# Residual rows and scattered expert additions go straight to an output declared with spare rows, without a scratch sum

## The chip, the cores and the metric

One core of one Trainium2 chip runs the kernel. The metric is the device time of one execution in microseconds (us), as a median of several runs; lower is better.

## The reference

A decoder layer on x of 2 x 1024 tokens with 256 features: a decayed linear attention, a cross attention over 154 context rows with 16 heads, and a mixture of experts. Only the end of the last part matters for this change:

```python
h   = layernorm(x)                         # x: 2048 rows x 256, after both attentions
g   = softmax(h @ gate_w.T)                # 8 experts; the two largest of g + gate_b are taken
out = x + shared_expert(h)                 # silu((h@sw1+sb1)*(h@sw3+sb3)) @ sw2 + sb2
for each token, for each of its 2 experts e:
    out[token] += g[token, e] * expert_e(h[token])
```

The result has 2048 rows of 256 f32, 2.10 MB.

## The kernel before

The kernel is written by hand: each engine has its own program (`@block.tensor`, `.scalar`, `.vector`, `.gpsimd`, `.sync`), and semaphores order them. The layer runs in stages. Up to about 410 us the attentions and the shared expert run; x stays in SBUF and collects their sums, in four chunks of 512 tokens.

The experts work by sorted rows. GpSimd (POOL) scatters the normalised row of each token twice, once for each of its experts, into the scratch DRAM tensor `xs` (L1502), where each expert has a region of its own. With a row go its token number and its gate weight. Places without a token are filled from a table of pad rows that carry numbers from 2048 upwards, so that what is computed for them lands in spare rows. The tensor `zs` in DRAM has ZROWS = 2048 + 8*128 + 7*128 = 3968 rows of 1 KB: 2048 for the tokens and 1920 spare ones.

`zs` is filled first. SP's queue copies x with the shared expert's part into it, one 512-row chunk a time (`base`, L1665; chunks 0, 1, 2 on semaphore `base_zs`, chunk 3 on `base_zs3`), and gives the spare rows some finite content from the input (L1681).

Then NS = 39 tiles of 128 sorted rows follow each other, `s` = 0 to 38, the first NA = 16 of them made from the first three chunks. For each tile SP reads 128 rows from `xs` (`read`, L1672, up to NR = 8 tiles ahead, held back by the landing of the addition eight tiles earlier, L1671); TensorE (PE) transposes (L689), multiplies with both first weights (L700), transposes the hidden rows (L710) and multiplies with the second weight (L720); VectorE (DVE) adds biases (L1421, L1425, L1436) and multiplies with the gate weight (L1439) into one of four buffers `sY`; POOL adds the 128 rows to `zs` with one indirect DMA that reads, adds and writes (L1583).

Two such additions may meet in a row of `zs` when they belong to two experts. So the addition of tile s waits for the landing of s-2 always, and for that of s-1 where the expert changes between the two (the value `need`; always for s = 1, 2 and 16). The landings count on two semaphores in turn, `to_zs[s % 2]`. DVE waits for the landing of s-4 before it refills `sY`.

When the last two additions have landed, SP (L1729) and ACT (L963) copy half of the 2048 rows each from `zs` to the output `out`, and ACT waits for both copies. That is the end of the kernel.

Of the kernel before, what the change touches and what calls it, by code (L numbers as in the profile page):

```python
# [7 lines left out]
ALU = mybir.AluOpType  # L8
ACT = mybir.ActivationFunctionType
AX = mybir.AxisListType  # L10
F32 = mybir.dt.float32
U8 = mybir.dt.uint8
I32 = mybir.dt.int32
U32 = mybir.dt.uint32

P = 128
B = 2
S = 1024
D = 256
N = B * S  # L20
NT = N // P
NCH = 4
CT = 512
# [9 lines left out]
NS = (2 * N + NE * (P - 1)) // P  # L33
# [3 lines left out]
ZROWS = N + NE * P + 7 * P  # L37
NU = NT // 2
NR = 8
# [118 lines left out]
    return v.rearrange("p (a n) -> p a n", a=1).broadcast_to([P, n, NE])  # L158


def decoder(nc, A, xs, zs, out):
    with ExitStack() as ctx:
        def sb(name, shape, dt=F32):
            return ctx.enter_context(nc.sbuf_tensor(name, shape, dt))

        def sem(name):
            return ctx.enter_context(nc.semaphore(name))
# [9 lines left out]
        x = sb("x", [P, NT, D])  # L177
# [80 lines left out]
        xsl = R2[:, 0:NR * XW].rearrange("p (s n) -> p s n", s=NR)  # L258
# [21 lines left out]
        sY = R1[:, 11264:12288].rearrange("p (s n) -> p s n", s=4)  # L280
# [18 lines left out]
        in_row = [sem(f"in_row{i}") for i in range(NR)]  # L299
        to_xs = sem("to_xs")  # L300
        pad_xs = sem("pad_xs")
        base_zs = sem("base_zs")
        base_zs3 = sem("base_zs3")
        to_zs = [sem(f"to_zs{i}") for i in range(2)]
        to_out = sem("to_out")

        zeroed = signal("zeroed", ["ones", "cnt", "pad0", "pad1"])
        stat = signal("stat", [(kc, i, n) for kc in NORMS for i in range(4) for n in range(2)])
# [33 lines left out]
        def added(s):  # L342

            return 16 * (s // 2 + 1)
# [397 lines left out]
        def _(e):  # L742
            w = Waits(e)
# [212 lines left out]
                if s >= 1:  # L956
                    hidden_turned(s - 1)

            half = N // 2
            outr = out.rearrange("b s d -> (b s) d")  # L960
            for s in (NS - 2, NS - 1):
                e.wait_ge(to_zs[s % 2], added(s))
            e.dma_start(outr[half:N, :], zs[half:N, :]).then_inc(to_out, 16)  # L963
            e.wait_ge(to_out, 32)

        @block.vector
        def _(e):
            w = Waits(e)
# [462 lines left out]
            def results(s):  # L1431
                u = bank["y", s]
                w.wait_ge(full[u.i], u.filled)
                if s >= 4:
                    w.wait_ge(to_zs[s % 2], added(s - 4))
                e.tensor_tensor(sY[:, s % 4, :], pb[:, u.i, 0:D], eb[:, bass.ds(b_reg[s] * 960 + 2 * F, D)], ALU.add  # L1436
                                ).then_inc(free[u.i], 1)
                w.wait_ge(free[u.i], u.drained)
                e.tensor_scalar(sY[:, s % 4, :], sY[:, s % 4, :], xsl[:, s % NR, D + 1:D + 2], None, ALU.mult  # L1439
                                ).then_inc(*yrow.next(s))  # L1440

            for s in range(NS + 2):
                if s < NS:
                    hidden(s)
                if s == 0:
                    shared_out(3, 1)
                if s >= 2:
                    results(s - 2)
                if s == 2:
                    late_ends()  # L1450
                if s == 3:
                    late_jumps()
                if s == 4:
                    late_slots()

        @block.gpsimd
        def _(e):
            w = Waits(e)
# [42 lines left out]
            def scatter_rows(c, k, i):  # L1501
                e.indirect_dma_start(  # L1502
                    out=xs, out_offset=bass.IndirectOffsetOnAxis(ap=pos[:, c, k, i:i + 1].bitcast(U32), axis=0),
                    in_=xn[:, NORMS.index((3, c)) % 2, i, :], in_offset=None).then_inc(to_xs, 16)
# [31 lines left out]
            d = bank["mix", 3, 1]  # L1536
# [30 lines left out]
                scatter_rows(3, 0, i)  # L1567
            second_weights(3)

            w.wait_ge(base_zs, 64)  # L1570
            for s in range(NS):
                w.wait_ge(slots.sem, slots["early" if s < NA else "late"])
                v = e.value_load(need[0:1, s:s + 1], min_val=16, max_val=16 * (NS + 4)) if s not in (0, 1, 2, NA) else None  # L1573
                w.wait_ge(yrow.sem, yrow[s])
                if s >= 2:
                    w.wait_ge(to_zs[s % 2], added(s - 2))
                if s in (1, 2, NA):
                    w.wait_ge(to_zs[(s - 1) % 2], added(s - 1))
                elif s:
                    e.wait_ge(to_zs[(s - 1) % 2], v)  # L1580
                if s == NA:
                    w.wait_ge(base_zs3, 16)
                e.indirect_dma_start(  # L1583
                    out=zs, out_offset=bass.IndirectOffsetOnAxis(ap=xsl[:, s % NR, D:D + 1].bitcast(U32), axis=0),
                    in_=sY[:, s % 4, :], in_offset=None, compute_op=ALU.add).then_inc(to_zs[s % 2], 16)
                if s < 4:
                    scatter_rows(3, 1, s)

        @block.sync
        def _(e):  # L1590
            w = Waits(e)
            xv = A["x"].rearrange("b (t p) d -> p (b t) d", p=P)

            def fetch_side(t):
                s = t % 2
                if t >= 2:
                    d = bank["s", t - 2, 2, 0]
                    w.wait_ge(free[d.i], d.drained)
                e.dma_start(fs[:, s, :, :], A["fside"][t]).then_inc(in_fs[s], 16)

            def fetch_mask(t):
                s = t % 2
                if t >= 2:
                    w.wait_ge(masked.sem, masked[t - 2, heads_of(t - 2)[-1]])
                else:
                    for q in range(4):
                        d = bank["div", 3, q]
                        w.wait_ge(full[d.i], d.filled)
                e.dma_start(mk[:, s, :, :], A["mask"][t]).then_inc(in_mk[s], 16)
# [32 lines left out]
            for key in (("con", B - 1, 2), ("pj", 3, "q", 1)):  # L1642
                d = bank[key]
# [7 lines left out]
            def fetch_w2():  # L1651
                for ex in range(NE):
                    e.dma_start(ew2[:, ex * 768:ex * 768 + 512].rearrange("p (k n) -> p k n", k=2),
                                A["L0_ffn_w2"][ex, 0:256].rearrange("(k p) n -> p k n", p=P)).then_inc(in_ew2, 16)
                    e.dma_start(ew2[0:96, ex * 768 + 512:ex * 768 + 768], A["L0_ffn_w2"][ex, 256:352]
                                ).then_inc(in_ew2, 16)

            def fetch_eb(lo, hi):
                e.dma_start(eb[:, lo * 960:hi * 960], A["ebias"][:, lo * 960:hi * 960].broadcast_to(
                    [P, (hi - lo) * 960])).then_inc(in_ew, 16)  # L1660

            def base(c, to):
                d = bank["so", c, 1, 1]
                w.wait_ge(free[d.i], d.drained)
                e.dma_start(zs[c * CT:c * CT + CT, :].rearrange("(t p) d -> p t d", p=P),  # L1665
                            x[:, 4 * c:4 * c + 4, :]).then_inc(to, 16)

            def read(s):
                if s >= NR:
                    w.wait_ge(to_zs[s % 2], added(s - NR))  # L1670
                v = e.value_load(sei[0:1, 1, s:s + 1], min_val=0, max_val=XROWS - P)  # L1671
                e.dma_start(xsl[:, s % NR, :], xs[bass.ds(v, P), :]).then_inc(in_row[s % NR], 16)  # L1672

# [2 lines left out]
            for t in range(NT):  # L1676
                if t >= 2:
                    fetch_side(t)
                fetch_mask(t)
                if t == 4:  # L1680
                    e.dma_start(zs[N:ZROWS, :], A["x"].rearrange("b s d -> (b s) d")[0:ZROWS - N, :]  # L1681
                                ).then_inc(base_zs, 16)
                if t == 13:
                    base(0, base_zs)

            for r in range(2):
                d = bank["s", NT - 1, 2, r]
# [2 lines left out]
            fetch_w13(0, 3)  # L1690
            w.wait_ge(masked.sem, masked[NT - 1, (0, H)])
            fetch_w2()
            base(1, base_zs)
            fetch_eb(0, 3)
            w.wait_ge(scaled.sem, scaled[NT - 1, 1])
            fetch_w13(3, 6)
            d = bank["pT", 7, 1, 4]
            w.wait_ge(full[d.i], d.filled)
            fetch_w13(6, NE)
            for i in range(2):  # L1700
                for r in range(2):
                    d = bank["av", 7, 1, i, r]
# [5 lines left out]
            w.wait_ge(slots.sem, slots["early"])  # L1708
            for s in range(NR):
                read(s)  # L1710
            base(2, base_zs)
            w.wait_ge(prows.sem, prows[0])
            for ex in range(NE):
                v = e.value_load(prow[0:1, ex:ex + 1], min_val=ex * RG, max_val=ex * RG + N)
                e.dma_start(xs[bass.ds(v, P), :], A["pad"][ex * P:(ex + 1) * P, :]).then_inc(pad_xs, 16)
            base(3, base_zs3)
            for s in range(NR, NA):
                read(s)
            w.wait_ge(slots.sem, slots["late"])
# [2 lines left out]
            for s in range(NA, NS):  # L1722
                read(s)

            half = N // 2
            outr = out.rearrange("b s d -> (b s) d")
            for s in (NS - 2, NS - 1):
                w.wait_ge(to_zs[s % 2], added(s))
            e.dma_start(outr[0:half, :], zs[0:half, :]).then_inc(to_out, 16)  # L1729


def layout(inputs):
# [64 lines left out]
```

## Time and profile before

| | us |
|---|---|
| three runs | 605.31, 605.50, 607.53 |
| median | 605.5 |
| the profiled execution's own time | 605.35 |
| its span in the trace (first to last instruction or landing) | 603.5 |
| granted TensorE clock over the span, share of full | 0.991 |

Busy shares of the span: PE 94%, DVE 73%, ACT 52%, POOL 39%. The page cuts the span into 40 slices of 15.1 us; a digit is the busy share of a slice in tenths. The chain of work that ended last is followed back from the end; "issue" in it is time in which an engine waited for nothing that the profile shows. POOLq, SPq and ACTq are the sequencers of these engines, on which DMAs are issued.

### The profile page before, as it was taken

The page shows a single profiled execution, that of the slowest core. Times are in us where ns is not written, and L with a number is a line of the kernel's source. Part 1 is how long each engine was busy: PE and PEld are TensorE (multiplying, and loading weights), DVE is VectorE, ACT ScalarE, POOL GpSimd, SP SyncE. Part 2 cuts the span into 40 slices and gives each one's busy share as a digit, 9 for nine tenths or more (in the row PEclk, how much of TensorE's full clock was granted, in tenths as well). Part 3 has the DMA queues.
Part 4 walks back from the last instruction along what each step waited for, and adds up shares of the span by engine and source line. Part 5 has one row for each costly group of instructions (what it writes and reads, how often), then busy time and mean ns, then how long its engine had stood idle before and what let it go on. Part 6 is the DMA issues. An engine that isn't in the chain of part 4 may idle for free.

```text
span 603.5 us, 11032 instructions
## 1 busy us (share of the span) xinstructions
PE 569.9 (94%) x3625; PEld 434.0 (72%) x3625; DVE 437.6 (73%) x817; ACT 311.7 (52%) x985; POOL 234.3 (39%) x227
## 2 busy tenths in 40 slices
PE   4999999999999999999999999999999999999990
PEld 2546657787788878688787868777777777777770
DVE  3999999999686979749697498566575555555550
ACT  2642424388869794877959569424233232322320
POOL 2010010227453745367342684262354334333341
PEclk9999999999999999999999999999999999999996
DMA  9910004246250502415133149764544343443425
GB/s 305 364 46 2 1 1 167 87 166 236 106 207 5 194 18 93 153 35 211 36 115 123 45 146 304 240 247 121 136 96 71 57 68 62 62 71 54 63 28 163
DMA packets 36647, 71.00 MB, mean 118 GB/s; under 512 B 5184, under 2 KB 29472, under 8 KB 34080
## 3 DMA queue, kind: packets, MB, share of 16 engines
q1 hardware_dynamic: 28272, 59.18, 29.7%
q0 software_dynamic: 7152, 9.34, 9.3%
q10 hardware_dynamic: 1168, 1.78, 0.9%
q8 instruction: 30, 0.49, 0.3%
q14 instruction: 25, 0.20, 0.1%
HBM read 58.86 MB, written 17.48 MB: 126 GB/s over the span
## 4 chain that ended last, share of the span: by engine, by line
PE 35%; DVE 23%; issue 17%; DMA 14%; POOL 5%; ACT 2%; POOLq 2%; DVEq 0%; SPq 0%
DMA zs_dram<-R 13%; PE pb L571 7%; DVE R L1035 6%; PE pb L471 6%; PE pb L521 4%; PE pb L606 4%; PE pb L488 4%; PE pb L537 4%; DVE R L1058 3%; PE pb L618 2%; DVE R L1013 2%; DVE mx L1121 1%; POOLq L1573 1%; PE pb L541 1%; DMA xs_dram<-xn,pos 1%
## 5 line engine op out<-in xcount | busy, mean ns | idle before, releaser
L819 ACT ACTIVATE R<-R,mx 128x154 f32<-128x154 f32 x256 | 104.3, 414 | 0.0
L700 PE MATMUL pb<-R 128*128 x312 | 98.8, 460 | 0.3 <-ACT R L932 0.3
L1583 POOL DMA_INDIRECT zs_dram<-R x39 | 60.6, 1553 | 96.2 <-DMA zs_dram<-R 51.0
L936 ACT ACTIVATE R<-R 128x352 f32<-128x352 f32 x39 | 19.4, 497 | 116.7 <-DVE R L1429 110.8
L700 PEld LDWEIGHTS pb<-R 128*128 128x128 f32 x312 | 56.2, 190 | 25.4 <-issue 0.6
L471 PE MATMUL pb<-xnT,wq 128*128 128x256 f32 x256 | 58.0, 383 | 0.0
L720 PE MATMUL pb<-R 128*128 (+1 forms) x234 | 57.0, 380 | 0.0
L810 ACT ACTIVATE R<-pb,bq 128x256 f32<-128x256 f32 x64 | 30.0, 473 | 49.7 <-PE pb L471 49.7
L471 PEld LDWEIGHTS pb<-xnT,wq 128*128 128x128 f32 x256 | 47.8, 190 | 7.8 <-issue 1.2
L1502 POOL DMA_INDIRECT xs_dram<-xn,pos x32 | 31.9, 997 | 52.4 <-DVE pos L1217 44.0
L571 PE MATMUL pb<-wo,R 128*128 128x256 f32 x224 | 50.0, 380 | 0.6 <-DVE R L1145 0.6
L1477 POOL TENSOR_TENSOR sd<-mv,cst 128x4 f32<-128x4 f32 x12 | 12.2, 1020 | 98.6 <-DVE mv L983 98.5
L831 ACT COPY R<-pb 128x512 f32<-128x512 f32 x80 | 40.8, 616 | 16.8 <-PE pb L521 16.8
L819 ACT ACTIVATION_READ_ACCUMULATOR R<-R,mx 128x1 f32 x256 | 49.1, 192 | 0.0
L1103 DVE TENSOR_TENSOR R<-pb,R 128x924 f32<-128x924 f32 (+1 forms) x48 | 45.2, 998 | 4.3 <-PE pb L488 3.3
L571 PEld LDWEIGHTS pb<-wo,R 128*128 128x128 f32 x224 | 42.3, 190 | 7.6 <-DVE R L1145 1.0
L1114 DVE SCALAR_TENSOR_TENSOR R<-R 128x2464 f32<-128x2464 uint8 (+1 forms) x17 | 47.0, 2766 | 0.0
L720 PEld LDWEIGHTS pb<-R 128*128 128x128 f32 (+1 forms) x234 | 41.6, 191 | 4.3 <-issue 0.2
L1121 DVE TENSOR_REDUCE mx<-R 128x16 f32<-128x2464 f32 (+1 forms) x17 | 43.6, 2565 | 0.4
L412 PE MATMUL pb<-xnT,R 128*128 128x512 f32 x96 | 43.0, 599 | 0.7 <-issue 0.7
L606 PE MATMUL pb<-xnT,sw 128*128 128x256 f32 (+1 forms) x192 | 43.5, 381 | 0.0
L1421 DVE TENSOR_TENSOR R<-pb,KV 128x352 f32<-128x352 f32 x39 | 20.4, 524 | 26.5 <-PE pb L700 21.6
(168 smaller groups left out, 1114.6 us busy)
## 6 DMA issues: line engine op xcount, KB each, us to landing
R<-in_fside_dram SPq DMA_DIRECT2D x16, 1232.0 KB, 5.6
R<-in_L_ffn_w_dram SPq DMA_DIRECT2D x16, 352.0 KB
R<-xs_dram SPq DMA_DIRECT2D x39, 129.0 KB, 2.1
R<-in_mask_dram SPq DMA_DIRECT2D x16, 308.0 KB, 2.9
KV<-in_ebias_dram SPq DMA_DIRECT2D x2, 1440.0 KB
zs_dram<-x SPq DMA_DIRECT2D x4, 512.0 KB
R<-in_L_ffn_w_dram SPq DMA_DIRECT2D x8, 256.0 KB, 4.3
zs_dram<-in_x_dram SPq DMA_DIRECT2D x1, 1920.0 KB
```

Source lines behind the costliest of these rows:

```text
L412: ins = e.matmul(pb[:, u.i, :], wqkv[:, k, col * P:(col + 1) * P], xnT[:, r, k, :], start=(k == 0), stop=(k == 1))
L471: ins = e.matmul(pb[:, u.i, 0:256], wq[:, k, j * P:(j + 1) * P], xnT[:, r, k, cols], start=(k == 0), stop=(k == 1))
L571: ins = e.matmul(pb[:, u.i, 0:D], oT[:, j, q * P:(q + 1) * P], wo[:, j, :], start=(j == 0), stop=(j == 7))
L606: ins = e.matmul(pb[0:mw, u.i, q * 256:q * 256 + 256], wm[:, k, lo:lo + mw], xnT[:, r, k, cols], start=(k == 0), stop=(k == 1))
L700: ins = e.matmul(pb[:, u.i, 0:F], xsT[:, s % 2, k, :], ew13[:, bass.ds(w_reg[s] * 1408 + q * 704 + k * F, F)], start=(k == 0), stop=(k == 1))
L720: ins = e.matmul(pb[:, u.i, 0:D], sT[0:mw, s % 2, m, :], ew2[0:mw, bass.ds(w_reg[s] * 768 + m * D, D)], start=(m == 0), stop=(m == 2))
L819: ins = e.activation(att[t % 3][:, h, :], att[t % 3][:, h, :], ACT.Exp, bias=mx[:, a4, 1, h:h + 1], accum_out=mx[:, a4, 2, h:h + 1])
L831: e.copy(pT[:, hf, 2 * k:2 * k + 2, :], pb[:, u.i, :].rearrange("p (i q) -> p i q", i=2)).then_inc(free[u.i], 1)
L1103: e.tensor_tensor(att[t % 3][:, 2 * lo:2 * hi, :].rearrange("p (r h) k -> p r h k", r=2), pb[:, u.i:u.i + 2, 0:n * SK].rearrange("p r (h k ...
L1114: e.scalar_tensor_tensor(out=att[t % 3][:, lo:hi, :], in0=mk[:, s, lo:hi, :], scalar=-BIG, in1=att[t % 3][:, lo:hi, :], op0=ALU.mult, op1= ...
L1121: e.tensor_reduce(mx[:, a4, 0, lo:hi], att[t % 3][:, lo:hi, :], AX.X, ALU.max).then_inc(*topped.next((t, hs, 0)))
L1583: e.indirect_dma_start(out=zs, out_offset=bass.IndirectOffsetOnAxis(ap=xsl[:, s % NR, D:D + 1].bitcast(U32), axis=0), in_=sY[:, s % 4, :], ...
```

## The change

`zs` is gone. The output is declared with all 3968 rows, and the copies of x, the filling of the spare rows and the 39 additions name `out` where they named `zs`. The first 2048 rows of the output are taken as a view when the arrays are handed back, outside the device program. The semaphores are renamed (`base_zs` to `base_out`, `to_zs` to `to_out`); waits and their values stay as they were. The two copies at the end, ACT's waits ahead of them and ACT's wait for both are removed. SP's program ends with waits for the chunk copies and the last two additions.

```diff
-        base_zs = sem("base_zs")
-        base_zs3 = sem("base_zs3")
-        to_zs = [sem(f"to_zs{i}") for i in range(2)]
-        to_out = sem("to_out")
+        base_out = sem("base_out")
+        base_out3 = sem("base_out3")
+        to_out = [sem(f"to_out{i}") for i in range(2)]
...
-            half = N // 2
-            outr = out.rearrange("b s d -> (b s) d")
-            for s in (NS - 2, NS - 1):
-                e.wait_ge(to_zs[s % 2], added(s))
-            e.dma_start(outr[half:N, :], zs[half:N, :]).then_inc(to_out, 16)
-            e.wait_ge(to_out, 32)
...
                 e.indirect_dma_start(
-                    out=zs, out_offset=bass.IndirectOffsetOnAxis(ap=xsl[:, s % NR, D:D + 1].bitcast(U32), axis=0),
-                    in_=sY[:, s % 4, :], in_offset=None, compute_op=ALU.add).then_inc(to_zs[s % 2], 16)
+                    out=out, out_offset=bass.IndirectOffsetOnAxis(ap=xsl[:, s % NR, D:D + 1].bitcast(U32), axis=0),
+                    in_=sY[:, s % 4, :], in_offset=None, compute_op=ALU.add).then_inc(to_out[s % 2], 16)
...
-                e.dma_start(zs[c * CT:c * CT + CT, :].rearrange("(t p) d -> p t d", p=P),
+                e.dma_start(out[c * CT:c * CT + CT, :].rearrange("(t p) d -> p t d", p=P),
                             x[:, 4 * c:4 * c + 4, :]).then_inc(to, 16)
...
-                    e.dma_start(zs[N:ZROWS, :], A["x"].rearrange("b s d -> (b s) d")[0:ZROWS - N, :]
-                                ).then_inc(base_zs, 16)
+                    e.dma_start(out[N:ZROWS, :], A["x"].rearrange("b s d -> (b s) d")[0:ZROWS - N, :]
+                                ).then_inc(base_out, 16)
...
-            half = N // 2
-            outr = out.rearrange("b s d -> (b s) d")
+            w.wait_ge(base_out, 64)
+            w.wait_ge(base_out3, 16)
             for s in (NS - 2, NS - 1):
-                w.wait_ge(to_zs[s % 2], added(s))
-            e.dma_start(outr[0:half, :], zs[0:half, :]).then_inc(to_out, 16)
+                w.wait_ge(to_out[s % 2], added(s))
...
-    out = nc.dram_tensor("out_0_dram", (B, S, D), F32, kind="ExternalOutput").ap()
+    out = nc.dram_tensor("out_0_dram", (ZROWS, D), F32, kind="ExternalOutput").ap()
     xs = nc.dram_tensor("xs_dram", (XROWS, XW), F32, kind="Internal").ap()
-    zs = nc.dram_tensor("zs_dram", (ZROWS, D), F32, kind="Internal").ap()
-    decoder(nc, aps, xs, zs, out)
+    decoder(nc, aps, xs, out)
     r = _run(nc, [arrays], core_ids=[0])
-    return r.results[0]["out_0_dram"]
+    return r.results[0]["out_0_dram"][0:N].reshape(B, S, D)
```

## Rows read from the trace of the kernel before

**Rows 1.** The page's head and slices: busy tenths, granted clock, DMA share, traffic.
```profile
span 603.5 us, 11032 instructions
...
PE   4999999999999999999999999999999999999990
...
DMA  9910004246250502415133149764544343443425
GB/s 305 364 46 2 1 1 167 87 166 236 106 207 5 194 18 93 153 35 211 36 115 123 45 146 304 240 247 121 136 96 71 57 68 62 62 71 54 63 28 163
```

**Rows 2.** Busy time by stretch: PE, PEld, DVE, ACT, POOL, clock, DMA share, GB/s.
```profile
434.00:470.00 36.00, 36.00 (x164) 26.47 (x163) 23.22 (x62) 9.59 (x33) 18.15 (x13) 1.00 0.46 87
...
500.00:550.00 50.00, 50.00 (x227) 36.85 (x226) 27.73 (x60) 14.23 (x48) 18.59 (x12) 1.00 0.41 62
...
594.00:603.50 9.50, 0.00 (x0) 0.00 (x0) 0.00 (x0) 0.00 (x0) 0.00 (x0) 0.50 0.61 221
```

**Rows 3.** Timeline, 588 to 604 us: start, duration, engine, line, idle before.
```profile
588.34 1.55 POOL L1583 DMA_INDIRECT zs_dram<-R  x1 [0.77 <-DVE R L1439]
...
589.01 0.48 DVE L1439 TENSOR_SCALAR R<-R 128x256 f32<-128x256 f32 x1
590.54 1.55 POOL L1583 DMA_INDIRECT zs_dram<-R  x1 [0.65 <-issue]
594.39 0.56 SPq L1729 DMA_DIRECT2D out_dram<-zs_dram  x1
594.41 0.60 ACTq L963 DMA_DIRECT2D out_dram<-zs_dram  x1
```

**Rows 4.** DMA issues by line; the last column is us from issue to landing.
```profile
out_dram<-zs_dram SPq DMA_DIRECT2D x1, 7.8
out_dram<-zs_dram ACTq DMA_DIRECT2D x1, 8.7
```

**Rows 5.** The chain that ended last: start us, us, what; landings of additions.
```profile
439.57 4.91 DMA zs_dram<-R
...
506.12 4.43 DMA zs_dram<-R
...
566.08 3.59 DMA zs_dram<-R
...
586.02 3.79 DMA zs_dram<-R
590.31 1.77 POOLq L162
```

**Rows 6.** POOL's timeline, 493 to 524 us: additions, with the idle time before each.
```profile
493.48 1.55 POOL L1583 DMA_INDIRECT zs_dram<-R  x1 [2.67 <-DVE R L1439]
498.12 1.55 POOL L1583 DMA_INDIRECT zs_dram<-R  x1 [3.10 <-DVE R L1439]
502.75 1.55 POOL L1583 DMA_INDIRECT zs_dram<-R  x1 [3.08 <-DMA zs_dram<-R]
506.12 1.55 POOL L1583 DMA_INDIRECT zs_dram<-R  x1 [1.82 <-DVE R L1439]
511.31 1.55 POOL L1583 DMA_INDIRECT zs_dram<-R  x1 [3.64 <-DMA zs_dram<-R]
514.56 1.55 POOL L1583 DMA_INDIRECT zs_dram<-R  x1 [1.70 <-DVE R L1439]
518.77 1.55 POOL L1583 DMA_INDIRECT zs_dram<-R  x1 [2.67 <-DMA zs_dram<-R]
```

**Rows 7.** DVE's timeline, 505 to 519 us: the last step ahead of an addition.
```profile
505.50 0.35 DVE L1439 TENSOR_SCALAR R<-R 128x256 f32<-128x256 f32 x1
509.71 0.35 DVE L1439 TENSOR_SCALAR R<-R 128x256 f32<-128x256 f32 x1
513.93 0.35 DVE L1439 TENSOR_SCALAR R<-R 128x256 f32<-128x256 f32 x1
518.14 0.35 DVE L1439 TENSOR_SCALAR R<-R 128x256 f32<-128x256 f32 x1
```

**Rows 8.** SP's queue by time: the copies of x, reads of sorted rows.
```profile
296.06 0.38 SPq L1665 DMA_DIRECT2D zs_dram<-x  x1
...
418.78 0.43 SPq L1665 DMA_DIRECT2D zs_dram<-x  x1
...
432.72 0.58 SPq L1665 DMA_DIRECT2D zs_dram<-x  x1
439.58 126.81 SPq L1672 DMA_DIRECT2D R<-xs_dram  x31
```

**Rows 9.** The page's totals of HBM traffic.
```profile
HBM read 58.86 MB, written 17.48 MB: 126 GB/s over the span
```

More of the change, by code:

```diff
@@ L158, in by_end, with decoder @@
     return v.rearrange("p (a n) -> p a n", a=1).broadcast_to([P, n, NE])
-def decoder(nc, A, xs, zs, out):
+def decoder(nc, A, xs, out):
     with ExitStack() as ctx:
@@ L1434, in results @@
                 if s >= 4:
-                    w.wait_ge(to_zs[s % 2], added(s - 4))
+                    w.wait_ge(to_out[s % 2], added(s - 4))
                 e.tensor_tensor(sY[:, s % 4, :], pb[:, u.i, 0:D], eb[:, bass.ds(b_reg[s] * 960 + 2 * F, D)], ALU.add
@@ L1568, in _ @@
             second_weights(3)
-            w.wait_ge(base_zs, 64)
+            w.wait_ge(base_out, 64)
             for s in range(NS):
@@ L1575, in _ @@
                 if s >= 2:
-                    w.wait_ge(to_zs[s % 2], added(s - 2))
+                    w.wait_ge(to_out[s % 2], added(s - 2))
                 if s in (1, 2, NA):
-                    w.wait_ge(to_zs[(s - 1) % 2], added(s - 1))
+                    w.wait_ge(to_out[(s - 1) % 2], added(s - 1))
                 elif s:
-                    e.wait_ge(to_zs[(s - 1) % 2], v)
+                    e.wait_ge(to_out[(s - 1) % 2], v)
                 if s == NA:
-                    w.wait_ge(base_zs3, 16)
+                    w.wait_ge(base_out3, 16)
                 e.indirect_dma_start(
-                    out=zs, out_offset=bass.IndirectOffsetOnAxis(ap=xsl[:, s % NR, D:D + 1].bitcast(U32), axis=0),
-                    in_=sY[:, s % 4, :], in_offset=None, compute_op=ALU.add).then_inc(to_zs[s % 2], 16)
+                    out=out, out_offset=bass.IndirectOffsetOnAxis(ap=xsl[:, s % NR, D:D + 1].bitcast(U32), axis=0),
+                    in_=sY[:, s % 4, :], in_offset=None, compute_op=ALU.add).then_inc(to_out[s % 2], 16)
                 if s < 4:
@@ L1669, in read @@
                 if s >= NR:
-                    w.wait_ge(to_zs[s % 2], added(s - NR))
+                    w.wait_ge(to_out[s % 2], added(s - NR))
                 v = e.value_load(sei[0:1, 1, s:s + 1], min_val=0, max_val=XROWS - P)
@@ L1680, in _ @@
                 if t == 4:
-                    e.dma_start(zs[N:ZROWS, :], A["x"].rearrange("b s d -> (b s) d")[0:ZROWS - N, :]
-                                ).then_inc(base_zs, 16)
+                    e.dma_start(out[N:ZROWS, :], A["x"].rearrange("b s d -> (b s) d")[0:ZROWS - N, :]
+                                ).then_inc(base_out, 16)
                 if t == 13:
-                    base(0, base_zs)
+                    base(0, base_out)
             for r in range(2):
@@ L1692, in _ @@
             fetch_w2()
-            base(1, base_zs)
+            base(1, base_out)
             fetch_eb(0, 3)
@@ L1710, in _ @@
                 read(s)
-            base(2, base_zs)
+            base(2, base_out)
             w.wait_ge(prows.sem, prows[0])
@@ L1715, in _ @@
                 e.dma_start(xs[bass.ds(v, P), :], A["pad"][ex * P:(ex + 1) * P, :]).then_inc(pad_xs, 16)
-            base(3, base_zs3)
+            base(3, base_out3)
             for s in range(NR, NA):
@@ L1723, in _ @@
                 read(s)
-            half = N // 2
-            outr = out.rearrange("b s d -> (b s) d")
+            w.wait_ge(base_out, 64)
+            w.wait_ge(base_out3, 16)
             for s in (NS - 2, NS - 1):
-                w.wait_ge(to_zs[s % 2], added(s))
-            e.dma_start(outr[0:half, :], zs[0:half, :]).then_inc(to_out, 16)
+                w.wait_ge(to_out[s % 2], added(s))
 def layout(inputs):
```

## The prediction

> **What bounds the kernel now.** I read the busy tenths by slice first [rows 1]: PE is at nine tenths in every slice from the second on and at nothing in the last. The table by stretch says the same for the expert stage: 36.00 of 36.00 us and 50.00 of 50.00 us busy at the full clock [rows 2]. So up to some 588 us the pace is PE's, one tile per 4.2 us: DVE's last step for a tile starts at 505.50, 509.71, 513.93 and 518.14 [rows 7], 12.64 us for three tiles, 4.21 each. Then I read the end. In the last 9.5 us no engine is busy, while the DMA share is 0.61 [rows 2], the heaviest it has been since the expert stage began. The timeline names what it is: DVE finishes the last tile at 589.01 + 0.48 = 589.49, POOL issues the last addition at 590.54, its landing lets SP issue a copy at 594.39 and ACT one at 594.41, and nothing follows in the timeline [rows 3]. They land 7.8 and 8.7 us after their issue [rows 4], the later at 594.41 + 8.7 = 603.11; the span ends at 603.5 [rows 1], 0.39 us later.
>
> Last the chain that ended last. Through the expert stage it runs over additions [rows 5], which looks as if POOL's DMAs were the bound. POOL's own timeline corrects this [rows 6]: 493.48 to 518.77 is 25.29 us for six tiles, 4.215 each, the pace of PE. Some gaps are longer (498.12 to 502.75 is 4.63; 506.12 to 511.31 is 5.19) and the next ones shorter (3.37, 3.25): where the expert changes, an addition waits for its predecessor's landing, comes up to 1 us late, and the next catches up. The landing time shifts POOL inside the stage, and counts only at the end.
>
> **The copies at the end.** Removed from the path that sets the end: everything from the copies' issue at 594.39 to the later landing at 603.11, that is 8.72 us [rows 3, 4]. Nothing covers it, since all engines are idle there [rows 2]. What is late next is the last addition itself: SP's waits pass at 594.39 as before. What came after the last landing, 0.39 us, I keep; bounds are 0 and, if the end costs what it costs to go from the last landing to the next issue on POOL (586.02 + 3.79 = 589.81 landed, 590.54 issued: 0.73 us [rows 3, 5]), 0.34 us more. New span: 603.5 - 8.7 = 594.8.
>
> The copies have no work behind which they shrink or move, so no gain is given back later; this is the unusual case of a removed DMA with full value. What the fixed cost of a landing is does not matter, as the trace has the whole duration.
>
> One rule gives another size. The Trainium skill, DMA: Bandwidth & Descriptors, section "Anatomy of one DMA — SWDGE (gpsimd) path", fits a DMA's time as 2.0 us plus its bytes over 436 GB/s. For the two copies together, 2.10 MB on the same engines, that is an estimate of 6.8 us, and the kernel would take 1.9 us more than by the rows. The page's fit is for GpSimd's DMAs and the trace has 8.7 us for these two, so the trace is used.
>
> **The additions, now into the output.** 39 additions keep their size (128 rows of 1 KB), their queue, order and waits. Before, landings took 4.91 us early in the stage, 4.43, 3.59 and 3.79 later, counted from POOL's issue [rows 5]; the last one 594.39 - 590.54 = 3.85 [rows 3]. No row shows an addition into an output tensor. The nearest rows are these same additions, and I take no difference, since `zs` and the output are both DRAM tensors with 1 KB rows, and the copies show that the output is written by the same queues. Bounded by the spread in the rows: -0.2 us (3.59 for 3.79) to +1.1 us (4.91 for 3.79). How often does it count at the end? The last addition (s = 38) had its data at 589.49 and was issued at 590.54, after s = 36 had landed at 589.81 [rows 3, 5]: it waited for s-2. So the end holds two landings in series, and a change of d in each moves it by 2d: -0.4 to +2.2 us. Inside the stage d is hidden by the catching up described above, as long as it is under about 1.5 us (below).
>
> **The copies of x and the spare rows.** The same transfers with another target. The first addition needs chunks 0 to 2 and the spare rows; the last of them is issued at 418.78, some 16 us before the first addition. Chunk 3 is issued at 432.72 [rows 8] and needed by s = 16, the addition at 502.75 [rows 6], 70 us later. Cost 0, hidden by the expert stage's start; were a copy to take 16 us longer, it would delay POOL from the first addition.
>
> **SP's new waits, ACT's removed ones.** SP's last read is issued by 439.58 + 126.81 = 566.39 [rows 8]. Its waits for the chunks come then, with semaphores long reached, and nothing is queued behind them. They are over 28 us before the end: 0. The waits for the last two additions were there already. ACT's wait was the end and is gone with the copies.
>
> **Around the span.** The profiled execution took 605.35 us, 1.85 more than its span, and stands 0.15 under the median of the three runs (605.5). The output grows from 2048 to 3968 rows. If what lies around the span grew with it, 1.85 x 3968/2048 = 3.58, 1.7 us more. But two copies of the 2.10 MB took 8.7 us on the device [rows 4], so the 1.85 us hold no handling of the output's bytes. I take 0 and keep 1.7 as the upper end.
>
> **Sum.** 605.35 - 8.72 = 596.6 for an execution like the profiled one, 596.7 beside the median. Traffic: the page's HBM read falls from 58.86 MB by 2.10 and the written from 17.48 by 2.10 [rows 9].
>
> **The rivals.**
>
> *Slower: landings in the output take longer, and the additions become the bound.* The trace's tightest pattern is a change of expert every third tile: 506.12, 511.31, (514.56, 518.77) and so on. In it two of three gaps are full landings in series, about 4.85 us each (the mean of 5.19 and of 4.64 and 4.63, weighted to the former), against 3 x 4.215 = 12.65 us of PE for three tiles [rows 6]. 2 x (4.85 + d) = 12.65 gives d = 1.5 us from which POOL falls behind PE. Beyond it 13 such groups lose 26 x (d - 1.5), and the end 2d. At d = 2.0 that is 13 + 4 = 17 us, less the 8.7 removed: some 614. Breaking even with the gain, and over it by 3 us, lies at d = 1.8. For it speaks only that no row shows these writes. Against it: the landings hardly depend on what else is moved, 4.43 us at 506.12 amid the reads and 3.85 for the very last [rows 3, 5], so 1.8 us would be half again of all that a landing takes.
>
> The Trainium skill (DMA: Bandwidth & Descriptors, section "Latency and other measured facts") has a memory access at 0.2 us on average and 2 us under high load, and says that this makes most of a DMA's fixed cost; by that rule a busy memory would add 1.8 us, just what this rival needs. The traffic does not rise with the change, and the trace disagrees that it is near such a load: 62 GB/s in the stage [rows 2].
>
> *The end doesn't come earlier.* Something else that ends with the copies, or work of the runtime for the output, would fill the time: 604 to 606. Against it: the timeline has no instruction behind 594.41 but the copies [rows 3]. A part of it, the time around the span grown with the output, gives 596.7 + 1.7 = 598.4.
>
> *A modest slowdown of landings.* d between 0.3 and 1.1 us: 597.3 to 598.9, by the end alone.
>
> **How the numbers follow.** Forecast, the copies' full price with landings as they were: 0.84, at 596.7, own range 595.9 to 597.4 (landings 0.2 shorter or 0.3 longer, twice, and the end's 0.3). Modest slowdown or more time around the span: 0.10, 597.3 to 598.9. The end doesn't come earlier: 0.03. Additions become the bound: 0.03. The range reaches from 595.6, a little under the first, for the runs' own spread (605.31 against 605.50), to 599.0. About 0.5%, 3 us, is what a measurement of this kernel can tell from no change. Faster by more, under 602.5: 0.94; within: 0.03; slower: 0.03.
>
> **What the profile after would show.** Right: the last addition issued near 590.5 and the span ending 4.2 us behind it, at 594.8; no DMA with `out` as target but the chunk copies, the spare rows and POOL's 39; landings of 3.6 to 4.9 us in the chain; PE at 50 of 50 us in mid-stage. Wrong in a step: landings above 5 us, gaps on POOL that no longer average 4.2 us and PE under full (the slower rival); a span of 595 but a time of 598 or more (around the span); an end that stays more than 1 us behind the last landing (the 0.39 us). The prediction is most exposed to the landing time, which it takes from a tensor of another kind.

## The result and the profile after

The changed kernel took 601.7 us as a median of five runs (599.76 to 602.58), beside 605.5 for the kernel before (605.29 to 607.53): ratio 0.993, 95% interval [0.9905, 0.9955]. It is faster by 3.8 us; 8.8 were forecast, and 601.7 lies above the stated range.

The profiled execution took 599.76 us, with a span of 597.9. First the page: its head, busy tenths, DMA and traffic, as in [rows 1] and [rows 9], and the DMA issues that write the output.

```profile
span 597.9 us, 11030 instructions
...
PE   4999999999999999999999999999999999999993
...
DMA  8920004254450512415123238783545343433423
...
HBM read 56.76 MB, written 15.38 MB: 121 GB/s over the span
...
out_dram<-x SPq DMA_DIRECT2D x4, 512.0 KB, 3.2
out_dram<-in_x_dram SPq DMA_DIRECT2D x1, 1920.0 KB, 8.7
```

Both directions of HBM traffic fell by 2.10 MB, the copies. Busy time by stretch answers to [rows 2] (columns as there):

```profile
434.00:470.00 36.00, 36.00 (x164) 26.56 (x163) 23.60 (x61) 9.51 (x32) 18.26 (x13) 1.00 0.44 78
500.00:550.00 50.00, 50.00 (x227) 36.87 (x226) 27.74 (x60) 14.26 (x48) 18.59 (x12) 1.00 0.41 63
594.00:597.90 3.90, 0.00 (x0) 0.00 (x0) 0.00 (x0) 0.00 (x0) 0.00 (x0) 0.50 0.00 0
```

The stage is as it was, with PE busy throughout. The new thing is the last line: for the last 3.9 us no engine works and *no DMA moves a byte*. POOL's timeline and the landings of the additions (x39, the last column is us from issue to landing) answer to [rows 3] and [rows 5]:

```profile
588.12 1.55 POOL L1575 DMA_INDIRECT out_dram<-R  x1 [0.78 <-DVE R L1431]
590.29 1.55 POOL L1575 DMA_INDIRECT out_dram<-R  x1 [0.61 <-issue]
...
out_dram<-R POOLq DMA_INDIRECT x39, 3.8
```

The last addition is issued at 590.29 (590.54 before) and by its 3.8 us lands at 594.1. The span ends 3.8 us after that, where 0.39 us had been forecast. Line 162 opens the `with` statement around the whole program, right below the function's first line; to it the profile puts what closes the program block, where all engines meet. The view of that line in the changed kernel (duration in ns min/median/max, then start):

```profile
...
L162 PEldq DRAIN  x1: 1830/1830/1830, 586.4 to 586.4; - x1
L162 DVEq DRAIN  x1: 516/516/516, 588.8 to 588.8; - x1
L162 POOLq DRAIN  x1: 7646/7646/7646, 590.1 to 590.1; - x1
...
L162 SPq DRAIN  x1: 7/7/7, 594.4 to 594.4; - x1
L162 SPq EVENT_SEMAPHORE  x1: 17/17/17, 597.9 to 597.9; - x1
```

Each engine drains before the meeting. POOL's drain starts at 590.1 and lasts 7.65 us, to 597.7; SP, whose waits for the landings are over, is ready at 594.4 and waits for POOL. SP's waits say the same from the other side (us in total, times, longest; PEq stands as the releaser's name, though PE's drain ended at 588.2):

```profile
SPq L80 <- DMA out_dram<-R: 28.5, 2, 26.4
SPq L162 <- PEq L162: 3.5, 1, 3.5
```

The same drain is in the trace of the kernel before, in the same view:

```profile
L162 POOLq DRAIN  x1: 7646/7646/7646, 590.3 to 590.3; - x1
...
L162 ACTq COMPARE_BRANCH  x1: 42/42/42, 603.1 to 603.1; - x1
```

There it ended at 590.31 + 7.65 = 597.96, while the copies ran until 603.11. It was hidden behind what the change removes.

### The profile page after: what moved, and what is told of

It is laid out like the page before. It is cut to its first block, busy times and chain, and to the rows that moved or that the text cites. A ratio compares the mean times of both kernels' runs of the same rounds, so it can differ in the third digit from the quotient of the medians.

```text
span 597.9 us, 11030 instructions
## 1 busy us (share of the span) xinstructions
PE 569.8 (95%) x3625; PEld 434.0 (73%) x3625; DVE 437.9 (73%) x817; ACT 311.9 (52%) x985; POOL 234.5 (39%) x227
## 4 chain that ended last, share of the span: by engine, by line
PE 45%; DVE 23%; issue 14%; DMA 9%; POOL 4%; ACT 2%; POOLq 1%; DVEq 0%; SPq 0%
PE pb L699 7%; DMA out_dram<-R 7%; PE pb L570 7%; DVE R L1027 6%; PE pb L470 6%; PE pb L520 4%; PE pb L605 4%; PE pb L487 4%; PE pb L536 4%; PE pb L719 3%; DVE R L1050 3%; PE pb L617 2%; DVE R L1005 2%; DVE mx L1113 1%; PE pb L540 1%
## 5 line engine op out<-in xcount | busy, mean ns | idle before, releaser
L1575 POOL DMA_INDIRECT out_dram<-R x39 | 60.6, 1553 | 97.4 <-DMA out_dram<-R 53.4
## 6 DMA issues: line engine op xcount, KB each, us to landing
KV<-in_ebias_dram SPq DMA_DIRECT2D x2, 1440.0 KB, 10.5
```

The lines of the kernel that those rows point to most:

```text
L1575: e.indirect_dma_start(out=out, out_offset=bass.IndirectOffsetOnAxis(ap=xsl[:, s % NR, D:D + 1].bitcast(U32), axis=0), in_=sY[:, s % 4, :] ...
```

## The experiments

The theory that the experiments start from (A): POOL's drain was hidden behind the copies and now ends last. Rivals: (B) the larger output costs time in the stage or around the span; (C) additions land later in the output than in the scratch tensor.

For all of them one number frees the comparison of what happens earlier in a run: the time from the issue of the last addition to the end of the span. Before it is 603.54 - 590.54 = 13.00 us, after 597.94 - 590.29 = 7.65 us.

**The drain left out.**

```diff
-        block = ctx.enter_context(nc.Block())
+        block = ctx.enter_context(nc.Block(no_gpsimd_drain=True))
```

> The changed kernel, with the drain of POOL's queue at the end of the program block left out (the block is opened with no_gpsimd_drain=True); SP still waits for the landing of the last two additions. In the profile of the changed kernel the last landing is at 594.10 us, but a drain of POOL that starts at 590.06 lasts 7.65 us, to 597.71, and the span ends at 597.94. Theory A (this drain was hidden behind the two copies and now sets the end): the span falls to about 594.5 (0.4 us behind the landing) in the profile, the time to about 596.4, and the spread of the five runs of the changed kernel (599.76 to 602.58) shrinks to a few tenths. Rival B (the larger output costs time in the stage or around the span): the time stays near 600 to 602 although the drain is gone, with more than 1.9 us between span and time. Rival C (additions land later in the output in the undisturbed runs): span varies as before, with landings over 4.5 us.

Measured: 597.3 us beside 606.3, ratio 0.9863 [0.9828, 0.9898]. The profiled execution took 596.17 us with a span of 594.4:

```profile
590.11 1.55 POOL L1575 DMA_INDIRECT out_dram<-R  x1 [0.62 <-issue]
...
SPq L162 <- PEq L162: 0.2, 1, 0.2
```

SP's wait at the meeting went from 3.5 to 0.2 us, and from the last addition's issue to the end it is 4.29 us. Theory A holds, with the size it had named. The time around the span is 1.8 us as before, so B's larger output costs nothing there. Nor does it in the stage: from the first addition to the last are 155.57 us in the kernel before (434.97 to 590.54) and 155.53 in the changed kernel (434.76 to 590.29). The spread did not shrink as theory A had it (596.17 to 597.81, and later up to 600.1), so the drain isn't what makes runs differ.

**The changed kernel once more.** No edit.

> The changed kernel itself, beside the others on the same chip, for a second record of its end. Theory A: POOL's drain starts near 590.1 and ends last, by 597.7 or later; where the time is above 600, the drain's record is longer than 7.65 us by the same amount, with the last landing still near 594.1. Rival C: where the time is above 600, the last additions land later than 594.5.

Measured: 601.1 us beside 606.3, ratio 0.9919 [0.9892, 0.9945], single runs from 598.99 to 603.96. The profiled execution took 601.31 us, 1.55 us more than the first. Its drain has the same 7.65 us, and the last addition was issued at 591.84, 1.55 us later than in the first: the end is 7.65 us long again. A's and C's guesses on what makes a run longer both fall for this one: its 1.55 us lie ahead of the stage. The first matmuls with the 512-wide operand (line 411 of the changed kernel; PE busy us and mean ns) in the first profile of the changed kernel:

```profile
L411 PE MATMUL pb<-xnT,R 128*128 128x512 f32 x24 | 10.5, 595 | 0.7 <-issue 0.7
```

and in this one, with the same line's shortest, median and longest in ns:

```profile
L411 PE MATMUL pb<-xnT,R 128*128 128x512 f32 x24 | 12.0, 662 | 0.7 <-issue 0.7
...
L411 PE MATMUL pb<-xnT,R x24: 592/592/1191, 12.8 to 24.2; 128*128 128x512 f32 x24
...
L411 PEld LDWEIGHTS pb<-xnT,R x5: 286/337/337, 12.8 to 15.5; 128*128 128x128 f32 x5
```

At 12.8 us the same 24 matmuls begin with one of 1191 ns where the first profile has 667; two of 1061 and one of 744 follow, and the rest take 592 as there. The weight loads between the long ones (the last line, the view cut off at 15.7 us) take 337 ns where 190 is usual. I take this as TensorE at 1.2 GHz for these few and at 2.4 GHz after. That is argued from durations: the profile's row of the granted clock says 1.00 for 13 to 16 us in both profiles. What speaks for it is the execution with 512 copied rows, below, where the weight loads take the same 337 ns while the row says 0.50.

The group takes 12.0 - 10.5 = 1.5 us more. VectorE's first reciprocal behind it (L1061) starts at 35.55 us in place of 34.27, 1.3 us later, and the last addition 591.84 - 590.29 = 1.55 us later: nothing is caught up. The execution with a drain behind tile 30, below, has 13.6 us in the same group, 3.1 us more than the first, and its last addition comes 2.5 us later. What decides how long the first matmuls stay long was not tested.

**The drain begun late.** POOL first waits for the landing of its last two additions.

```diff
                 if s < 4:
                     scatter_rows(3, 1, s)
+            for s in (NS - 2, NS - 1):
+                w.wait_ge(to_out[s % 2], added(s))
```

> The changed kernel with POOL waiting for the landing of its last two additions (about 594.1) ahead of the end of its program, so that the drain begins with nothing in flight. Tells what the drain's 7.65 us are made of. If it takes a fixed time from its start: it ends at 594.2 + 7.65 = 601.9, the span is 602.1, the time about 604. If it ends a fixed 3.6 us behind the last landing: span 597.9, as in the changed kernel, time 599.8 or more. If it only waits for what is in flight: span near 594.6 to 595.5, time 596.5 to 597.4. Rival B, by which the drain has no part in the end: the time of the changed kernel, whatever the drain does.

Measured: 602.2 us beside 606.3, ratio 0.9942 [0.9917, 0.9967]; in the profile:

```profile
592.42 1.55 POOL L1575 DMA_INDIRECT out_dram<-R  x1 [0.60 <-issue]
...
L162 POOLq DRAIN  x1: 5867/5867/5867, 596.4 to 596.4; - x1
```

With nothing in flight the drain still takes 5.87 us, and the end has grown to 10.04 us. So it does not wait for landings. In the other profiles its 7.65 us begin while POOL still works on the last addition: 590.06 + 7.65 = 597.71, and POOL is done with it at 590.29 + 1.55 = 591.84, 5.87 us before. The drain costs 5.87 us behind POOL's last instruction. That is neither the 7.65 from its start nor "3.6 behind the landing", and no wait for what is in flight: all three guesses missed. The end is 2.4 us longer than the changed kernel's by the traces and the median 1.2 us (602.2 beside 601.1), with single runs 3 and 5 us apart; the size is taken from the traces.

**Scratch tensor as before, but hardly a copy.** One copy of 16 rows in place of two of 1024; the rest of the output is left unwritten.

```diff
...
-            e.dma_start(outr[half:N, :], zs[half:N, :]).then_inc(to_out, 16)
-            e.wait_ge(to_out, 32)
...
-            e.dma_start(outr[0:half, :], zs[0:half, :]).then_inc(to_out, 16)
+            e.dma_start(outr[0:16, :], zs[0:16, :]).then_inc(to_out, 16)
+            e.wait_ge(to_out, 16)
```

> The kernel before, with additions and copies of x still into the scratch tensor, and with the two copies of 1024 rows at its end replaced by one of 16 rows from SP (the rest of the output is left unwritten). It takes away the copies' time without touching the output's size or the target of the additions. SP's copy is issued at 594.4 and should land some 2 to 3 us later, by 597.4. Theory A: the drain, begun at 590.3, ends at 597.96 and sets the end: span 598.1, time 599.9 to 602, as the changed kernel. Rival B or C (the output tensor as a target, or its size, costs time): below the changed kernel by 2 us or more only if they and not the drain cost it; that would need the drain to be shorter here.

Measured: 600.8 us beside 606.3, ratio 0.9922 [0.9896, 0.9948], no different from the changed kernel's 601.1 on the same chip. The additions go into the scratch tensor here, and the output has its old size; the last addition was issued at 589.53, the drain again has 7.65 us, and the end is 597.19 - 589.53 = 7.66 us. B and C fall: target and size of the output cost nothing that can be seen.

**The kernel before without the drain, and the changed kernel without it again.** Both with the edit of the first experiment.

> The kernel before, copies and all, with the drain of POOL's queue at the end of the block left out. Theory A: there the drain ended at 597.96 us in the profile, over 5 us ahead of the later copy's landing at 603.11, so it was fully hidden: the time stays within 0.3% of the kernel before. If the drain had a price of its own also there (by holding up the engines' meeting at the end), the time falls by up to 5 us.

> The changed kernel without the end drain, once more, beside the kernel before without it: both differ only in the change itself, with no drain behind it. My prediction's sum then has to hold: 8.7 us between them, ratio 0.9856. A rival by which additions into the output cost something in the stage gives less than 8.7.

Measured: 605.6 us beside 605.7 for the kernel before, ratio 1.0004 [0.9985, 1.0024]: there the drain was free. The changed kernel without it took 598.0, ratio 0.9859 [0.9829, 0.989] to the kernel before, where my sum gives 596.7 / 605.5 = 0.9855. Between the two kernels without a drain the expectation had 8.7 us. The medians have 7.5, the means of the same runs 8.2, with single runs 5 to 6 us apart in each, so the runs alone can't tell 7.5 from 8.7. The ends of the profiles have 12.47 - 4.21 = 8.3 us. The 0.4 us missing there are no more than what the later copy took less, 8.1 us here where it had been 8.7:

```profile
out_dram<-zs_dram SPq DMA_DIRECT2D x1, 7.8
out_dram<-zs_dram ACTq DMA_DIRECT2D x1, 8.1
```

**A drain in the middle of the stage.**

```diff
                 if s < 4:
                     scatter_rows(3, 1, s)
+                if s == 20:
+                    e.drain()
```

> The changed kernel with a second drain on POOL, right behind the addition of tile 20. Tells whether the length depends on the DMAs issued since the last drain (67 would be cut to 18 for the one at the end). If it does: the end drain takes 1.5 to 2 us behind the last instruction in place of 5.87 and the span falls to about 594.6. If it is a fixed cost: both drains take 5.87 us behind the instruction ahead of them, the middle one delays additions 21 and 22 by some us that the next ones catch up, and the span stays at 598 to 600.

One run: 596.7 us, span 594.9. POOL's timeline around the middle drain and at the end, and the two drains (L1581 the one in the middle):

```profile
518.40 1.55 POOL L1575 DMA_INDIRECT out_dram<-R  x1 [2.67 <-DVE R L1431]
525.94 1.55 POOL L1575 DMA_INDIRECT out_dram<-R  x1 [5.99 <-issue]
527.79 1.55 POOL L1575 DMA_INDIRECT out_dram<-R  x1 [0.30 <-issue]
532.39 1.55 POOL L1575 DMA_INDIRECT out_dram<-R  x1 [3.04 <-DMA out_dram<-R]
...
590.10 1.55 POOL L1575 DMA_INDIRECT out_dram<-R  x1 [0.59 <-issue]
...
L1581 POOLq DRAIN  x1: 6412/6412/6412, 518.2 to 518.2; - x1
...
L162 POOLq DRAIN  x1: 4752/4752/4752, 589.9 to 589.9; - x1
```

The end drain went from 7.65 to 4.75 us, that is from 5.87 to 2.98 us behind POOL's last instruction (589.88 + 4.75 - 591.65). The expectation had 1.5 to 2 us for it. Its length depends on what POOL did since the last drain: 18 DMAs here, 71 in the others. From the last addition's issue to the end are 594.87 - 590.10 = 4.77 us, so this drain still ends a little behind the landing. The middle one cost POOL 4.62 us behind addition 20. Addition 21 came at 525.94 in place of about 523.0 (in the changed kernel it follows addition 20 by 4.61 us), and three tiles later all was caught up. PE was busy for 17.00 of the 17.00 us from 518 to 535.

**A smaller copy of 512 rows.** The diff is that of the 16 rows, with 512.

> The kernel before with one copy of 512 rows from SP at the end in place of two of 1024 (the rest of the output is left unwritten); the drain as it was. One size changed: 0.5 MB should land some 3.5 to 4.5 us after its issue at 594.4, at 597.9 to 598.9, about when the drain ends (5.87 us behind POOL's last instruction, 597.96). Theory A: the span ends 0.2 to 0.4 us behind the later of the two. If the copies' time and not a drain were all there is, a copy of 16 rows (landed at 595.45 where the addition before it landed at 593.3) would have ended the span at 595.9; it ended at 597.19.

One run: span 600.9, 602.7 us, in an execution whose last addition was issued late, at 592.96. The cause is in its trace (columns as in [rows 2]; the second line has the weight loads of that time, in ns):

```profile
418.00:421.40 3.40, 3.40 (x9) 2.69 (x9) 2.92 (x17) 0.00 (x0) 0.07 (x1) 0.50 0.65 197
...
L618 PEld LDWEIGHTS pb<-sw,hZ x12: 190/337/337, 417.9 to 421.8; 128*128 128x128 f32 x8, 96*128 96x128 f32 x4
```

From 418.0 to 421.4 us, just ahead of the expert stage, the granted clock was 0.50, that is 1.2 in place of 2.4 GHz; the changed kernel has 1.00 there. Twelve matmuls took 4.5 us in place of 2.8, and the first addition came at 437.32 in place of 434.76. Ahead of it PE had been busy for 11.14 of the 13.00 us from 405 to 418, beside 12.34 in the changed kernel; what made the clock fall was not tested. For the question here the end is what counts:

```profile
L162 POOLq DRAIN  x1: 7646/7646/7646, 592.7 to 592.7; - x1
...
SPq L162 <- DMA out_dram<-zs_dram: 3.4, 1, 3.4
SPq L162 <- PEq L162: 0.2, 1, 0.2
...
out_dram<-zs_dram SPq DMA_DIRECT2D x1, 512.0 KB, 3.9
```

The drain ended at 592.73 + 7.65 = 600.38, the copy landed at 600.47, and the span closed at 600.89, 7.93 us behind the last addition's issue. Half a megabyte could be copied for 0.3 us, in the drain's shadow.

**The drain moved, and once more left out.** One or two drains in the stage, at `s == 30` or `s in (15, 30)` in the edit above; the end drain stays.

> The changed kernel with one more drain on POOL behind the addition of tile 30; the end drain stays. With the drain behind tile 20 the middle one ended 4.62 us behind the instruction ahead of it (53 DMAs since the start) and the one at the end 2.98 us (18 DMAs since), against 5.87 us for 71: an estimate of 2.0 us + 0.055 us per DMA. Here 8 DMAs are left for the end: 2.4 us behind POOL's last instruction, near 594.0 where the last landing is seen at 593.9 to 594.1, so the end is set by the landing again: span 594.4 to 594.8, the time of the version without the drain within 0.1%. The middle drain should end 5.4 us behind addition 30 and be caught up before tile 36. If the end drain's length were not a matter of the DMAs since the last one, it would be 2.98 again or 5.87.

> The changed kernel with drains on POOL behind tiles 15 and 30. 48 DMAs before the first, 15 before the second, 8 before the end. By 2.0 us + 0.055 us per DMA: 4.6, 2.8 and 2.4 us behind the instruction ahead of each; span as with one drain behind tile 30.

> The changed kernel without the end drain, beside the version with a drain behind tile 30 on the same chip. If the two agree within 0.3%, the drain can be kept, moved into the stage where POOL has slack.

Measured, beside 605.8 for the kernel before: 598.7 us with a drain behind tile 30, ratio 0.9881 [0.986, 0.9901]; 597.1 without the end drain, ratio 0.9864 [0.9841, 0.9886]. The one run with two drains took 595.9. The drains in the profiles, first that with one, then that with two:

```profile
L1581 POOLq DRAIN  x1: 7002/7002/7002, 563.1 to 563.1; - x1
...
L162 POOLq DRAIN  x1: 4148/4148/4148, 592.6 to 592.6; - x1
```

```profile
L1581 POOLq DRAIN  x2: 4742/5406/6070, 497.3 to 560.1; - x2
...
L162 POOLq DRAIN  x1: 4287/4287/4287, 589.6 to 589.6; - x1
```

From the last addition's issue to the end: 4.16 us with one drain in the stage, 4.31 with two, 4.19 without the end drain. So the end is the same. The medians differ by 1.6 us, and the profiles by 2.9 us ahead of the end: the last addition was issued at 592.82 with one drain in the stage (the execution with the 13.6 us for the first matmuls told of above) and at 589.94 without the end drain. That the other runs with one drain were late for the same reason is not shown. Strictly, "within 0.3%" was met, 598.7 to 597.1 being 0.27%, but "within 0.1%" of the expectation was not, and it is the traces that show the ends equal. All drain lengths behind the instruction ahead of them:

| DMAs issued on POOL since the last drain | 71 | 63 | 53 | 48 | 18 | 15 | 8 |
|---|---|---|---|---|---|---|---|
| us since the last drain's end, or the start | 592 | 565 | 520 | 499 | 67 | 59 | 24, 27 |
| us behind that instruction | 5.87 | 5.22 | 4.62 | 4.30 | 2.98 | 2.96 | 2.38, 2.52 |

A line of 2.0 us and 0.055 us per DMA is within 0.35 us of all of them; for the run with two drains it had given 4.6, 2.8 and 2.4 us ahead of time, and 4.30, 2.96 and 2.52 were measured. The time since the last drain, which grows in the same order, fits worse: the drain gains 1.3 us over the 432 us between the columns of 18 and 48 DMAs, and 1.6 over the 93 us between those of 48 and 71. The first four columns hold the 32 scatters into `xs` beside the additions; by these four alone an addition costs (5.87 - 4.30) / 23 = 0.07 us. Why it grows so, and whether it counts DMAs or what they are cut into, was not tried: all the DMAs counted have 128 rows.

## Why the prediction was wrong

**What bounds the kernel now.** PE up to the end of the stage and the copies behind it: right. What I missed stood in a row that I had copied. [Rows 5] end with `590.31 1.77 POOLq L162`, a piece of POOL's sequencer at a line that is not in the tail's code. The prediction gives it no place. It is the first 1.77 us of a 7.65 us drain; the row ends at 592.08, where POOL's last addition instruction ends too, and the drain runs on for 5.87 us. I had looked at the timeline [rows 3], which shows busy engines and DMA issues, and took its silence between 594.4 and 603.1 for emptiness. One view of line 162 in the trace of before, shown above, gives the drain's end at 597.96.

**The copies at the end.** This is the step that failed: "What is late next is the last addition itself". Late next was the drain. The price of the copies, 8.72 us, was right; the gain is what remains over the next end. The term kept for the end, 0.39 us behind the last landing (with bounds of 0 and 0.73), was 3.8 in the changed kernel. The prediction had named this as a sign of being wrong: "an end that stays more than 1 us behind the last landing". The drain ends 5.87 us behind POOL's last instruction, whose own end is 590.54 + 1.55 = 592.09, so the copies could give back only 603.11 - 597.96 = 5.15 us, plus some 0.2 at the meeting. The profiles have 13.00 - 7.65 = 5.35. The missing 3.4 us came back in full when the drain was left out or shortened: 4.29, 4.21 and 4.19 us of end in the first case, where my 0.39 us behind a landing gives 3.85 + 0.39 = 4.24.

**The additions into the output.** No difference, right: 3.8 us to the landing as in [rows 5], and the same end with the scratch tensor. The slower rival, with its 1.8 us more per landing, and the modest one found nothing. The rule of the Trainium skill weighed there (DMA: Bandwidth & Descriptors, section "Latency and other measured facts", a memory access of 0.2 us on average and 2 us under high load) would have made landings of 3.8 + 1.8 = 5.6 us, an estimate. In the chain of the changed kernel's profile the longest landing of an addition is 4.48 us, so the trace doesn't bear it out.

On the other page rule, the fit of a DMA's time, the copies of this study give three sizes: 16 rows landed in 2.1 us, 512 rows (0.52 MB) in 3.9, and two of 1.05 MB together in 8.7 or 8.1. By the fit of the Trainium skill (DMA: Bandwidth & Descriptors, section "Anatomy of one DMA — SWDGE (gpsimd) path"), made for GpSimd's DMAs, they are estimated at 2.0, 3.2 and 6.8. It agrees at the small end and is short by about a fifth for these larger copies from DRAM to DRAM. The 598.6 us that its sum gave lies nearer to the 601.7, but by luck: the copies took the trace's 8.7 us, and what was missing was the drain.

**Copies of x, spare rows, SP's new waits, time around the span.** All 0, all right: the first two additions and the stage moved by 0.2 us, traffic fell by the 2.10 MB each way, and 599.76 - 597.94 is 1.8 us.

**The end that doesn't come earlier.** This rival had the mechanism in its first words, something else that ends with the copies, and I gave it 0.03 because the timeline has no instruction behind 594.41. I also had it all or nothing. What happened lies between: something that ended 5 us before the copies.

**The rest of the miss.** Of the 5.0 us between 596.7 and 601.7 the drain explains 3.4. The rest is which executions were met: the median lies 1.96 us above the profiled execution, 601.72 beside 599.76, the fastest of five, where for the kernel before it was 0.15, and the stage of the profiled execution ended 0.25 us earlier than before; 3.4 + 1.96 - 0.15 - 0.25 = 5.0. The range had 0.3 us for the runs' own spread, from the 0.15. Later runs of the kernel before spread from 603.7 to 610.0 us. The profiles show two causes: long first matmuls, worth 1.5 us at the last addition in one execution and 2.5 in another, and the stretch at half clock at 418 us, worth 2.7. Whether they are behind the runs that have no profile is open. A gain of 5.35 us was thus measured as 3.8 and as 5.3.

**What it takes to get the forecast.** The changed kernel with no end drain, or with a drain where POOL has slack, beats both kernels: ratios 0.9863, 0.9859, 0.9864 and 0.9881 to the kernel before.

## What to carry to other kernels

Before you credit the removal of the last thing in a program, list every engine's end: look at the sequencers' records at the line that closes the block, and take as the gain only the distance to the next-latest of them. Where GpSimd issues DMAs until the end, its drain is such an end, and a drain inserted earlier, where GpSimd waits anyway, takes over half of its length or a little more (5.87 us became 2.98, 2.52 and 2.38). A row in the chain that you can't explain is a question to ask of the trace, however short it is there.

## What the runs showed of the hardware that was not expected

- GpSimd's drain takes 5.87 us behind its last instruction after 71 DMAs of 128 rows, also when all of them have landed, and 2.4 to 3.0 us after 8 to 18.
- An extra drain of 4.6 us in the stage delayed the next addition by 2.9 us and the kernel by nothing; PE was busy for 17.00 of the 17.00 us around it.
- The first 24 matmuls with the 512-wide operand took 10.5, 12.0 or 13.6 us in three executions, by the number of them that took 1061 or 1191 ns in place of 592; of the 1.5 and 3.1 us more, 1.55 and 2.5 were left at the last addition.
- In one execution the granted clock fell to 0.50 from 418.0 to 421.4 us, and the last addition came 2.7 us later than in the changed kernel.
